# A decoder layer on one Trainium2 core: a reordered set-up, a schedule written out for the first and last groups, four `ML` buffers, four FFN banks and two half batches at the end

## What is computed

```python
# state space block, per sequence (cut)
xn = _rmsnorm(x, norm_w); proj = xn @ w_in.T          # value, gate, B, C, dt
val = silu(causal_conv4(val) + conv_b); ld = softplus(dt + dt_bias) * -exp(A_log)
M = einsum('blhn,bmhn->bhlm', c_c, b_c) * where(tril, exp(cum_i - cum_j), 0)
Y = M @ v_h + ... + Dv * v_h
out = (Y * silu(gate)) @ w_out.T
out = out + 0.5 * (memory_reads(out) @ w_read.T)
x = _layernorm(x + x + out)
# cross-attention
w = softmax(mask(q @ k.T / sqrt(128))); x = _layernorm(x + layernorm(w @ v @ Wo + bo) * g0 + beta0)
# FFN, 512 hidden channels, activations and weights quantised
h = bit_linear(x, w1); h = silu(depthwise_conv3(h) + b); x = _layernorm(x + bit_linear(h, w2))
```

## Time and profile before

| | |
|---|---|
| median of 3 executions | 953.85 us (952.76 to 954.5) |
| the profiled execution | 952.97 us |
| its span, first to last instruction | 951.2 us |
| mean granted TensorE clock | 0.937 |

### The profile page before, as it was taken

The page is one execution under the profiler, slowest core; times in us unless marked ns, Lnnn a source line. Parts: engine busy times, 40 slices in busy tenths (PEclk is TensorE's granted clock), DMA queues, the critical chain, the costliest instruction groups (busy, mean ns, idle before and its releaser), DMA issues.

```text
span 951.2 us, 21378 instructions
## 1 busy us (share of the span) xinstructions
PE 826.1 (87%) x7992; PEld 599.9 (63%) x7992; DVE 780.0 (82%) x2287; ACT 703.2 (74%) x1371; POOL 196.8 (21%) x237
## 2 busy tenths in 40 slices
PE   3279999999999999999999999999999999986432
PEld 2166776776767767776676776767767776744311
DVE  2165466989999999999999999999999999887745
ACT  1267768878788888888888888788888888754432
POOL 6100011212221212212131222222212212222121
PEclk9569999999999999999999999999999999997555
DMA  5112020202010111102020202010111102000000
GB/s 157 36 23 55 14 46 12 47 12 44 25 38 18 44 17 31 38 24 46 23 46 24 46 24 46 24 38 20 42 17 35 35 12 46 13 24 11 1 11 22
DMA packets 51300, 30.65 MB, mean 32 GB/s; under 512 B 40411, under 2 KB 42413, under 8 KB 50941
## 3 DMA queue, kind: packets, MB, share of 16 engines
q1 hardware_dynamic: 48844, 27.11, 12.4%
q10 hardware_dynamic: 2352, 2.18, 0.8%
HBM read 16.68 MB, written 4.19 MB: 22 GB/s over the span
## 4 chain that ended last, share of the span: by engine, by line
PE 51%; ACT 20%; DVE 16%; issue 7%; SPq 3%; POOL 1%; DMA 1%; ACTq 0%; POOLq 0%; DVEq 0%
PE pM L1228 8%; PE pP L1191 5%; ACT x L695 5%; PE pP L1193 4%; PE pP L1192 4%; DVE conv L887 3%; DVE fa L1046 3%; PE pDec L1218 3%; DVE fa L1044 2%; ACT L560 2%; PE pC L1249 2%; ACT fa L636 2%; PE pC L1334 2%; PE pA L1267 2%; PE pDec L1215 2%
## 5 line engine op out<-in xcount | busy, mean ns | idle before, releaser
L554 ACT ACTIVATE P<-pP 128x512 f32<-128x512 f32 x256 | 147.8, 597 | 32.9 <-PE pP L1193 30.1
L1191 PE MATMUL pP<-xn_hi,G_hi 128*128 128x256 f32 x512 | 158.8, 310 | 0.1
L1192 PE MATMUL pP<-xn_lo,G_hi 128*128 128x256 f32 x512 | 143.7, 281 | 0.0
L1193 PE MATMUL pP<-xn_hi,G_lo 128*128 128x256 f32 x512 | 143.6, 280 | 0.0
L1228 PE MATMUL pM<-P,xnT 128*64 128x512 f32 x512 | 133.7, 602 | 0.0
L1191 PEld LDWEIGHTS pP<-xn_hi,G_hi 128*128 128x128 f32 x512 | 97.4, 190 | 20.8 <-issue 13.0
L932 DVE TENSOR_TENSOR ML<-pM,Lm 128x512 f32<-128x512 f32 x128 | 87.6, 685 | 19.1 <-ACT Lm L560 10.1
L1192 PEld LDWEIGHTS pP<-xn_lo,G_hi 128*128 128x128 f32 x512 | 97.8, 191 | 1.4
L1193 PEld LDWEIGHTS pP<-xn_hi,G_lo 128*128 128x128 f32 x512 | 97.3, 190 | 0.0
L471 POOL TENSOR_TENSOR u<-u,fa 128x512 f32<-128x512 f32 x32 | 40.9, 1279 | 242.8 <-ACT u L641 242.8
L480 POOL TENSOR_TENSOR rs_c<-ve_c,half_pow 128x4 f32<-128x4 f32 x48 | 51.2, 1067 | 172.4 <-DVE nm_c L1018 102.4
(11 more groups left out here) (214 smaller groups left out, 2070.5 us busy)
## 6 DMA issues: line engine op xcount, KB each, us to landing
v_nat<-vT SPq DMA_DIRECT2D x256, 32.0 KB, 2.1
x_in<-in_x SPq DMA_DIRECT2D x16, 256.0 KB, 2.9
x_res<-in_x SPq DMA_DIRECT2D x16, 256.0 KB, 2.7
ctxT<-in_ctx_t SPq DMA_DIRECT2D x16, 256.0 KB, 3.0
out_x<-x SPq DMA_DIRECT2D x16, 256.0 KB, 2.0
P<-in_wc ACTq DMA_DIRECT2D x1, 1024.0 KB, 7.5
P<-in_wb SPq DMA_DIRECT2D x1, 1024.0 KB, 8.2
fa<-in_w_t ACTq DMA_DIRECT2D x1, 256.0 KB
```

Of the source, the lines that this page charges most:

```text
L554: act.activation(flat(P[:, half, 2 * pair:2 * pair + 2, :]), pP[k % 2][:, :], ACT.Copy)\
L1191: pe.matmul(dst, w_hi, x_hi, start=True, stop=False)
L1192: pe.matmul(dst, w_hi, x_lo, start=False, stop=False)
L1193: return pe.matmul(dst, w_lo, x_hi, start=False, stop=True)
```

## The change

The arithmetic stays the same, and every full group is still 8 sequences. Five things change.

1. **Set-up.** SP loads `x` of group 0 first, then the norm weight and the value and gate weights, then the B weights in two halves; ACT loads the identity and the C weights in two halves; all other loads, 16 of which ACT issued before, are on SP's queue. The 16 products `G` go to four banks of their own (`pDec`, `pM`, `pY`, `pD`), four heads at a time, between the first steps of group 0. ACT waits for `s_first` alone ahead of `norm_weight(0)`; the wait for POOL's tables stands at the steps that use them (`place_cum`, `place_v`, `decay`), and `memory_mask` behind `conv_bias(1, 1)`.
2. **Lists.** `iterations` and `run` are gone. Each engine has a `fill()` written out for the first groups, a `body(g)` for `g` from 4 to 11, and a `drain()` written out for the last ones. They hold the same steps on the same engines.
3. **`ML` has four buffers** instead of two.
4. **Late batches.** Stages C and D work on batches of `LATE` tiles: 15 of four tiles, and for the last group two of two tiles, numbered 15 and 16, the first of which needs only the first half of `Yg`.
5. **FFN banks.** The four chunks of `ffn_up` of batch 16 go to `pD`, `pA`, `pP0` and `pP1`.

```diff
+SIZES = (4,) * 16
+LATE = (4,) * 15 + (2, 2)
+ML_DEEP = 4
...
-            (id_f[:, :], ident), (nw[:, :], norm_w), (wvg[:, 0:JJ, :], w_val), (wvg[:, JJ:2 * JJ, :], w_gate),
+        first_loads = [(nw[:, :], norm_w), (wvg[:, 0:JJ, :], w_val), (wvg[:, JJ:2 * JJ, :], w_gate)]
...
+        def ffn_bank(d, c):
+            return (pD, pA, pP[0], pP[1])[c] if d == LATE_BATCHES - 1 else pD
...
-            sp.dma_start(wb_s, wb).then_inc(s_head, 16)
             load_x(0)
+            for dst, src in first_loads:
+                sp.dma_start(dst, src).then_inc(s_first, 16)
+            for i in range(2):
+                heads = slice(HH * i, HH * i + HH)
+                sp.dma_start(wb_s[:, heads, :], wb[:, heads, :]).then_inc(s_head[i], 16)
...
             rms_apply(0)
-            act.wait_ge(s_dve0, DVE_FIRST)
+            act.wait_ge(s_first, FIRST_LOADED)
...
+            def head_products(b):
+                if b % 2 == 0:
+                    pe.wait_ge(s_head[b // 2], 32)
+                for k in range(4):
+                    h = 4 * b + k
+                    last = pe.matmul((pDec, pM, pY, pD)[b][:, 128 * k:128 * k + 128], wc_s[:, h, :], wb_s[:, h, :],
+                                     start=True, stop=True)
+                last.then_inc(g_mm, 1)
...
-                dve.wait_ge(y_mm.sem, y_mm.at(g, s - 1))
-                dve.tensor_tensor(ML[:, s % 2, :], pM[:, :], Lm[:, s % 2, :], ALU.mult)\
+                dve.wait_ge(y_mm.sem, y_mm.unit(unit - ML_DEEP))
+                dve.tensor_tensor(ML[:, ml_slot(g, s), :], pM[:, :], Lm[:, s % 2, :], ALU.mult)\
...
-            for g in range(-1, NG + 3):
-                body(g)
+            fill()
+            for g in range(4, 12):
+                body(g)
+            drain()
```

More of the change, by code:

```diff
@@ new lines, in copy_p @@
+                if n == 0 and half == 1 and pair == 0:
+                    act.wait_ge(g_mm, 4)
+                if pair == 0 and n > 0:
+                    last = min(half_seqs(n - 1) * (half + 1), seqs_in(n - 1)) - 1
+                    act.wait_ge(m_mm.sem, m_mm.unit(FIRST_UNIT[n - 1] + last))
+                act.activation(P[:, half, 2 * pair:2 * pair + 2, 0:w], pP[k % 2][:, 0:2 * w].rearrange("p (h l) -> p h l", h=2),
+                               ACT.Copy).then_inc(p_copied.sem, per_half(n))
@@ L799, in _, with stats @@
+            fill()
+            for g in range(4, 12):
+                body(g)
+            drain()
         @block.vector
         def _(dve):
-            def stats(chain, group, src, st, mv):
-                for t in range(T):
+            def stats(chain, group, tiles_in, src, st, mv):
+                for t in range(tiles_in):
                     last = dve.bn_stats(st[:, t, :], src[:, t, :])
@@ L1245, in head_values, with bank, transposed @@
-                last.then_inc(y_mm.sem, 1)
-            def transpose4(bank, src, ident_t):
-                for t in range(T):
-                    last = pe.transpose(bank[:, 128 * t:128 * t + 128], src[:, t, :], ident_t)
+                                     ML[:, ml_slot(g, s), hh * L:hh * L + L], start=True, stop=True)
+                last.then_inc(y_mm.sem, per_unit(g))
+            def bank(b, t):
+                return b[:, 128 * t:128 * t + 128]
+            def transposed(dst, src, count):
+                for t in range(count):
+                    last = pe.transpose(bank(dst, t), src[:, t, :], id_f[:, :])
@@ new lines, in body @@
+            def body(g):
+                decay(g - 1, 5)
+                scores(g - 1, 4)
+                head_values(g - 1, 2)
+                head_values(g - 1, 3)
+                ffn_up(g - 3, 3)
+                head_pair(g, 0, 2)
+                head_pair(g, 0, 3)
+                x1_transposed(g - 2)
+                decay(g - 1, 6)
+                scores(g - 1, 5)
+                queries(g - 2)
+                project(g, A_GATE[1], 3)
+                head_pair(g, 0, 4)
+                attention_scores(g - 2)
+                scores(g - 1, 6)
+                head_values(g - 1, 4)
+                head_values(g - 1, 5)
+                head_pair(g, 0, 5)
+                maxima_transposed(g - 3)
+                weights_transposed(g - 2)
+                decay(g - 1, 7)
+                cum_transposed(g)
+                scores(g - 1, 7)
+                attend(g - 2)
+                head_pair(g, 0, 6)
+                scales_spread(g - 3)
+                head_pair(g, 0, 7)
+                v_transposed(g, 0)
+                decay(g, 0)
+                head_pair(g, 1, 0)
+                head_pair(g, 1, 1)
+                v_transposed(g, 1)
+                keys(g - 1)
+                decay(g, 1)
+                scores(g, 0)
+                head_values(g - 1, 6)
+                head_values(g - 1, 7)
+                x_transposed(g + 1)
+                context_values(g - 1)
+                head_pair(g, 1, 2)
+                ffn_down(g - 3)
+                decay(g, 2)
+                scores(g, 1)
+                project_dt(g + 1)
+                head_pair(g, 1, 3)
+                output_projection(g - 1)
+                project(g + 1, A_VAL[0], 0)
+                head_pair(g, 1, 4)
+                head_pair(g, 1, 5)
+                memory_scores(g - 1)
+                quantised_transposed(g - 2)
+                decay(g, 3)
+                scores(g, 2)
+                project(g + 1, A_VAL[1], 1)
+                ffn_up(g - 2, 0)
+                memory_values(g - 1)
+                head_values(g, 0)
+                head_values(g, 1)
+                head_pair(g, 1, 6)
+                ffn_up(g - 2, 1)
+                memory_read(g - 1)
+                head_pair(g, 1, 7)
+                decay(g, 4)
+                scores(g, 3)
+                cum_sums(g + 1)
+                ffn_up(g - 2, 2)
+                head_pair(g + 1, 0, 0)
+                head_pair(g + 1, 0, 1)
+                project(g + 1, A_GATE[0], 2)
```

2601 lines of the change are left out of this document (2137 added, 464 removed).

## The result

The changed kernel takes 914.69 us (median of 4, 909.31 to 916.42) and the kernel before 953.78 on the same chip: a ratio of 0.9581, 95% interval 0.9538 to 0.9625. The forecast was 893.7 us, 870 to 913. It is faster as forecast, but 21 us of the forecast's 60 are missing, and the time lies just outside the range.

The account below looks back on a forecast made before the run. The prediction took PE to bound the middle, with start and end chains of waits. Start 36, middle 781 and end 74 sum to 891 us; with 1.8 and 0.9 for execution and median, 893.7 us, range 870 to 913.

Parts of the forecast that it names:

- Start: Up to the first product into pM: 36 us (26 to 45) against 69.3, with waits for tables and later weights removed.
- The rival of a late start: Start: late POOL tables, a longer ACT list or PE's low clock make it 46 us, total 904; chance 0.12.
- Middle: First pM product to last ML: 781 us (762 to 794) against 786.1, with PE's 759.1 us of work as floor.
- The 1.52 us that PE idles in each full group I leave as they are: Middle: PE's idle time in each 50.86 us group stays; up to 20 us go if two ML buffers caused it.
- the middle gets shorter too: Rival: PE's idle time goes with four ML buffers, middle 764 us, total 877; chance 0.14.
- I count these 3.9 us as won: Middle, between 835 and 855.38: PE's lost 3.9 us are regained because the last groups' lists are interleaved anew.
- slower: Rival: new lists make each sequence wait for the other engine, 0.68 us each, middle 852, total 965; chance 0.02.
- End: From the last ML to the finish: 74 us (66 to 88) against 95.8, from 17 + 34 + 20.5 + 2.4.
- The first and last parts: End: last ML to last Yg 17 us; batch 16's stage D alone 20.5 us, plus 2.4 for the store.
- The middle part: End, from the last Yg to the end of the last quantise: 34 us, set by DVE's list, against 47.3.
- the tenth for waits: End: one tenth added to DVE's work for waits, making its 31 us of work 34 after the last Yg.
- Half batches do not pay: Rival: halves cost DVE some 7 us more work; with waits of 30% the end is 87, total 907; chance 0.14.

Follow-up runs that it names:

- whole_x1_pool_memsets: Changed kernel with whole late batches, the loop's order to the end, r1's sum moved to POOL, and v_bd and ew memsets before POOL's first rsqrt: 889.57 us, ratio 0.9340.
- ml_two_deep_in_loop: Changed kernel, but in groups 4 to 11 DVE waits before each ML as if it had two buffers, not four: 929.12 us, ratio 0.9776.

## Why the prediction was right or wrong

**Start, 36 us (26 to 45): right, 39.2.** `xn_lo` was there at 16.0 instead of 13, and the later marks keep that distance: the transposes of `v_nat` at 38.2 instead of 35, `pM` at 39.2 instead of 36. DVE's cast behind POOL's memsets is the visible cause of 1.3 us of it, but with the cast early PE's first projection step waited for a load and started 0.2 us sooner only, so the cast is not what made `pM` late. POOL's tables ended at 27.5, under cover as forecast, and the clock was at 0.96. The rival of a late start did not come.

**Middle, 781 us (762 to 794): wrong, 795.4.** Two sentences failed. "The 1.52 us that PE idles in each full group I leave as they are": a group fell from 50.97 to 49.09 us, and the rival "the middle gets shorter too" was right in the loop, for 15 of the 20 us that it allowed in 13 groups. (Its reason, the two buffers, is not shown: before, DVE waited for ACT and not for `head_values`.) The step behind the sentence was to name PE as the bound because it is the busiest. The measured bound is DVE's list, and the earlier trace rows had shown 47.69 us of it in 50.86, with some 140 gaps that a busy share leaves out. "I count these 3.9 us as won": the new order of the last four groups was taken to be at least as good as the old one, and without a row for it. It cost 24.3 us against before and 36 us against the loop's own order, 15.4 of them work of DVE done sooner and 21.0 idle time of DVE. This term alone makes the miss: with it at its forecast, the span would have been 886. Part of it is the clock: the sum had the middle's clock at 1.00 throughout; behind PE's waits for `v_nat` it fell three times, to 0.96 over the stretch, an estimated 7 to 9 us. The rival "slower" had the right kind of mechanism, new lists that make engines wait, but looked for it in every group instead of in the last four.

**End, 74 us (66 to 88): right, 79.7.** The first and last parts came within 1 us. The middle part was 38.5 instead of 34: DVE's list of 30.6 us was as I had it (31), the tenth for waits was a quarter.

**The cover that the sum did not see.** The end was judged alone, and the experiments show that end and last groups trade with each other: of the 36 us by which the loop's order brings the last `ML` forward, 23 return in the end. From group 11's first `ML` to the last instruction the changed kernel takes 346.0 us (266.24 + 79.71) and the kernel before 337.8. There half batches, four banks and written lists together are 8 us dearer, not cheaper. All of the gain lies in the start (30.1 us) and in the loop (14.9).

**"Half batches do not pay"** (0.14) named the right cost, some 7 us of DVE's work (8.2 measured), and no place: in the written lists their removal cost 18 us, in the loop's order it gained 7.5. The Trainium skill, "VectorE: DVE Perf Modes", section "The TRN2 errata", advises wide tiles since each instruction pays a fixed latency; the two runs in the loop's order agree.

**What stays open.** How the 21 us of idle time in the written order divide: DVE's three waits at the falls of the clock are 11.6 us of it, but the run that took two of PE's three waits for `v_nat` away brought other waits and other falls, and no run had the written order at full clock. Whether four `ML` buffers would help the old order of the body. And the new set-up was never undone by itself: its 30 us are read from the two traces.

## What to carry to other kernels

The busiest engine need not be the bound: add one instruction to each candidate and see whether the loop grows by its length (0.67 us on DVE, nothing for 0.45 us on PE). An order written out for the last rounds is worth nothing until it has been timed against the loop's own order running empty, and a size edit such as half batches has to be judged in each of them, since its sign can turn. A wait of the matrix engine can cost more than its length, so the granted clock of each stretch belongs beside its waits. And before an idle stretch gets a second bank or buffer, look for the next thing in the same chain that has only one or two: here the gain of four banks ended at two `fa` buffers.

## What the hardware did that I had not expected

A DVE cast of 128x512 fp32 to fp32r, all in SBUF, takes 0.43 us when POOL is idle as it is issued (kernel before, at 16.75, and `whole_x1_pool_memsets`, where the weights landed late, at 9.6 us, just behind the last memset). Issued during a row of POOL memsets it ended 0.27 us after the last of the row, and took 6.01, 5.7 or 1.98 us by how much of the row was left; it did not get in between two memsets. The Trainium skill, "SBUF — State Buffer", section "Who interferes with whom", says that a cast in a two-port mode and a GpSimd instruction lock each other out for a whole instruction. The trace agrees on the lock (no row tells the cast's mode), and shows it held over a row of instructions: six memsets of 0.5 to 1.8 us began while the cast of 6.01 us was held.

Short waits of PE were dearer than their length. In `ml_two_deep_in_loop` PE waits 1.8 us in each of seven equal groups; in four of them the granted clock fell to the lower level for some 3 us soon after, in three it did not, and the four groups are 1.4 to 1.7 us longer.
